# A two-layer attention, FFN, SSD and mixture-of-experts kernel on one Trainium2 core: attention in row and column tiles of TensorE, softmax sums and decay rows on ScalarE, a held expert fetch

## What is computed

```
# gate: a two-way decayed scan over the tokens of a sample (four of them: L0_cond, L0_cond2, L1_cond, L1_cond2)
decay = exp(-exp(w)) * (0.5 + 0.5 * tf)           # one number for a channel and a sample
a = a * decay + ekv_t ; b = b * decay + ek_t      # forward and backward over t
num = nf + nb - ekv + euk * vf ; den = df + db - ek + euk
out = sigmoid(r) * (num / max(den, 1e-8)) * (0.8 + 0.2 * tf)
# L0 attention: 16 heads of 16 channels, causal
att = einsum('bhtd,bhsd->bhts', q, k) / sqrt(16) + mask
z = softmax(att) @ v ;  x = x + z @ Wo.T
# L0 feed-forward: ternary weights, 8-bit activations, 256 -> 1024 -> 256
# L1 attention: an SSD (Mamba-2) block, 64 heads of 8, chunks of 32
# L1 feed-forward: 8 experts, top 2, 256 -> 704 -> 256
for e in range(8):
    h = silu(x @ w1[e].T) * (x @ w3[e].T)
    out = out + h @ w2[e].T * expert_weight
```

## Time and profile before

| | us |
|---|---|
| median of 3 runs (827.2 to 828.41) | 827.82 |
| the profiled execution | 827.53 |
| its span on the chip | 825.7 |
| start, to the first scores | about 0 to 86 |
| attention | about 86 to 304 |
| feed-forward | about 304 to 400 |
| SSD block | about 400 to 585 |
| routing and first gather | about 585 to 616 |
| experts | about 616 to 803 |
| combining and output | about 803 to 825.7 |

### The profile page before, as it was taken

One profiled execution on the slowest core, in us unless ns is written; L12 is line 12 of the kernel. 1 busy time (PEld: TensorE's weight loads), 2 busy tenths in 40 slices (PEclk: granted clock), 3 DMA queues, 4 the chain that ended last, 5 costly groups with the idle time before them and its releaser, 6 DMA issues.

```text
span 825.7 us, 13424 instructions
## 1 busy us (share of the span) xinstructions
PE 617.2 (75%) x5534; PEld 483.4 (59%) x5534; DVE 455.6 (55%) x565; ACT 329.9 (40%) x582; POOL 279.5 (34%) x150
## 2 busy tenths in 40 slices
PE   0009768986887771656799989998639999999990
PEld 0005657875786671224556456556628889898980
DVE  5995899869779729666395534443531111111113
ACT  5342234433542533767456654554312212222210
POOL 0542474564573404530001964430010212122210
PEclk9999877757879855958699999999759999999995
DMA  9200000000000000000000000000186888888814
GB/s 360 76 0 0 1 0 2 0 1 1 1 1 1 5 34 1 1 0 1 0 2 2 2 2 2 2 3 2 48 315 244 293 329 289 323 295 311 311 69 163
DMA packets 18125, 72.14 MB, mean 87 GB/s; under 512 B 4304, under 2 KB 9552, under 8 KB 14224
## 3 DMA queue, kind: packets, MB, share of 16 engines
q1 hardware_dynamic: 15856, 65.24, 21.5%
q0 software_dynamic: 2208, 6.03, 1.9%
HBM read 66.16 MB, written 5.11 MB: 86 GB/s over the span
## 4 chain that ended last, share of the span: by engine, by line
PE 56%; DVE 31%; ACT 7%; issue 3%; DMA 2%; SPq 0%; POOL 0%; DVEq 0%; POOLq 0%; ACTq 0%
PE PS L1257 46%; DVE arena L845 5%; DVE arena L846 5%; PE PS L1294 3%; DVE nmx L945 2%; PE PS L1306 1%; DVE dmat L841 1%; DVE R L863 1%; PE PS L1477 1%; DVE arena L860 1%; DVE arena L850 1%; DVE peak L1021 1%; DVE arena L1017 1%; DVE arena L1247 1%; DVE arena L859 1%
## 5 line engine op out<-in xcount | busy, mean ns | idle before, releaser
L1257 PE MATMUL PS<-arena 128*128 128x128 f32 (+5 forms) x1940 | 240.3, 293 | 35.5 <-DVE arena L934 15.1
L1257 PEld LDWEIGHTS PS<-arena 128*128 128x128 f32 (+2 forms) x1940 | 204.6, 181 | 68.4 <-issue 40.5
L549 ACT ACTIVATE arena<-PS,nmx 128x128 f32<-128x128 f32 (+1 forms) x128 | 43.4, 422 | 120.1 <-DVE nmx L945 120.1
L1234 DVE TENSOR_TENSOR R<-arena,PS 128x128 f32<-128x128 f32 x23 | 6.6, 287 | 145.4 <-ACT arena L786 145.4
L452 POOL DMA_INDIRECT ypair<-arena,oid x23 | 22.8, 990 | 146.6 <-ACT arena L792 146.6
L1257 PE MATMUL PS<-arena,R 128*128 128x256 f32 (+1 forms) x276 | 67.9, 388 | 0.6 <-ACT arena L792 0.6
L1257 PE MATMUL PS<-A,arena 128*128 128x128 f32 (+1 forms) x96 | 27.9, 446 | 38.3 <-DVE A L868 37.9
L1257 PEld LDWEIGHTS PS<-arena,R 128*128 128x128 f32 (+1 forms) x276 | 48.7, 189 | 13.3 <-issue 8.6
L1306 PE MATMUL PS<-ident,arena 128*128 128x128 f32 x192 | 34.5, 329 | 27.9 <-ACT arena L533 27.2
L426 POOL TENSOR_TENSOR arena<-arena 128x1024 f32<-128x1024 f32 x16 | 37.8, 2368 | 44.9 <-DVE arena L1089 36.9
L1294 PE MATMUL PS<-arena 128*128 128x128 f32 (+1 forms) x176 | 50.9, 417 | 0.8 <-DVE arena L887 0.8
(11 more groups left out here) (261 smaller groups left out, 1180.3 us busy)
## 6 DMA issues: line engine op xcount, KB each, us to landing
arena<-in_moe SPq DMA_DIRECT2D x23, 1408.0 KB, 6.6
arena<-in_moe SPq DMA_DIRECT2D x23, 768.0 KB, 8.2
arena<-ypair SPq DMA_DIRECT2D x4, 512.0 KB, 5.4
inproj<-in_inproj SPq DMA_DIRECT2D x1, 1344.0 KB, 11.3
arena<-in_fT SPq DMA_DIRECT2D x1, 1024.0 KB, 5.3
...
R<-in_w2T SPq DMA_DIRECT2D x1, 1024.0 KB, 10.3
```

The lines of the kernel that those rows point to most:

```text
L549: sc.activation(pr[u % 2][:, j, 0:n], PS[:, 2 * (u % 2) + j // 2, (j % 2) * 256:(j % 2) * 256 + n], ACT.Exp, bias=nmx[:, u % 2, j:j + 1]). ...
L1257: last = mm(dst, l, r, start=(n == 0), stop=(n == len(pairs) - 1))
```

## The change

Six things:
- **Scores.** GpSimd's masked copies go. ScalarE writes q twice, once with the even heads kept and once with the odd (`qT[0]`, `qT[1]`, eight copies for four). A head's scores are then a matmul over the 32 partitions that hold it and its neighbour (rows 0, 32, 64 or 96), in the order 0, 2, 1, 3, so that neighbours in the list use other rows and another bank of PSUM. The mask is two bf16 matmuls of 256 columns for four of 128.
- **Values.** v is the stationary operand, padded with zeros to 32 channels a head (GpSimd's memset), and the turned probabilities are the moving one; four heads write the four 32-partition groups of one bank. The result is z already turned: `turn_z` and `zt_copy` go. `project` has four steps of 128 padded channels for two.
- **Softmax sums.** ScalarE's exponentials write their row sums (`accum_out`). VectorE inverts them for each two units (`inverse_sums`), TensorE turns and repeats the inverses in eight column-tile matmuls, ScalarE copies them (`turned_sums`), and VectorE's `normalise`, now 16 times for 8, multiplies.
- **Decay rows.** Line 841 goes from VectorE; ScalarE writes each decay row in four instructions of 256 (`decay`), into one of two buffers.
- **Down projection.** Its last matmul has 128 rows, with zeros in the upper half.
- **Fetches.** The fetches of blocks 1 to 3 wait for the first gather to land.

```diff
@@ sync: fetches
                 if b >= RING:
                     sp.wait_ge(S["pe_y"], b - RING + 1)
+                if b == 1:
+                    sp.wait_ge(ld_xin[0], 16)
@@ gpsimd
-            masked(0)
-            masked(1)
-            for u in range(32):
-                if u + 2 < 32:
-                    masked(u + 2)
-                f, k = divmod(u, FRAME)
-                if k >= 2:
-                    gate_add(f + 2, k - 2)
-                elif k == 0 and f:
-                    gate_add(f + 1, 3)
+            pool.wait_ge(S["dve_R"], 2)
+            pool.memset(vv[:, :, :, HD:VW], 0.0).then_inc(S["pool_pad"], 1)
+            for i in range(2, 8):
+                for k in range(4):
+                    gate_add(i, k)
@@ scalar
+            def decay(i):
+                m, c = divmod(i, 2)
+                act.wait_ge(S["dve_dec"], 1)
+                if i >= 2:
+                    act.wait_ge(S["dve_scan"], 2 * (i - 1))
+                for n in range(4):
+                    ct, b = divmod(n, 2)
+                    sc.activation(dmats[i % 2][:, n * T:(n + 1) * T], notfirst[:], ACT.Copy,
+                                  scale=dec[:, m, ct, 2 * c + b:2 * c + b + 1]).then_inc(S["act_decay"], 1)
                 sc.activation(ek[:, ct, :], ek[:, ct, :], ACT.Exp).then_inc(S["act_ek"], 1)
+                decay(ct)
             bonus(0)
             bonus(1)
+            decay(2)
-                              ACT.Exp, bias=nmx[:, u % 2, j:j + 1]).then_inc(S["act_exp"], 1)
+                              ACT.Exp, bias=nmx[:, u % 2, j:j + 1],
+                              accum_out=esum[:, u // 2 % 2, 4 * (u % 2) + j:4 * (u % 2) + j + 1]).then_inc(S["act_exp"], 1)
                 if u >= 1:
                     pt_copy(u - 1)
+                if u % 2 and u >= 3:
+                    turned_sums(u // 2 - 1)
+                if k == 3 and i + 3 < 8:
+                    decay(i + 3)
@@ vector
+            def inverse_sums(p):
+                dve.wait_ge(S["act_exp"], 8 * (p + 1))
+                done(v.reciprocal(rinv[:, p % 2, :], esum[:, p % 2, :]), "dve_rinv")
+            def normalise(p):
+                dve.wait_ge(S["act_rT"], p + 1)
+                o = 256 * (p % 2)
+                done(v.tensor_tensor(zT[p // 2 % 2][:, o:o + 256], PS[:, 6 + p % 2, 0:256], rT[:, p % 2, :], ALU.mult), "dve_zn")
+                if u % 2 and u >= 3:
+                    inverse_sums(u // 2 - 1)
                 done(v.tensor_reduce(nmx[:, u % 2, :], ...), "dve_max")
+                if u % 2 == 0 and u >= 4:
+                    normalise(u // 2 - 2)
@@ tensor
+                for j in (0, 2, 1, 3):
+                    r = 32 * (2 * (g % 2) + j // 2)
+                    mm(PS[:, 2 * (u % 2) + j // 2, (j % 2) * 256:(j % 2) * 256 + n], qT[j % 2][r:r + 32, ch, ct, t:t + P],
+                       kT[r:r + 32, ct, b * T:b * T + n], start=(j % 2 == 0), stop=False)
+                for k in range(tt + 1):
+                    for j in range(4):
+                        last = mm(PS[32 * j:32 * j + 32, 6 + p % 2, o:o + P], vv[:, 2 * b + k, 4 * g + j, :],
+                                  pt[u % 2][:, (j * (tt + 1) + k) * P:(j * (tt + 1) + k + 1) * P], start=(k == 0), stop=(k == tt))
+                if u % 2:
+                    pe.wait_ge(S["dve_rinv"], p + 1)
+                    for h in range(8):
+                        j, o = h % 4, 256 + 128 * (h // 4)
+                        last = mm(PS[32 * j:32 * j + 32, 6 + p % 2, o:o + P], rinv[:, p % 2, h:h + 1].broadcast_to([P, VW]), ident[:],
+                                  start=True, stop=True)
@@ tensor: down_block
-                last = acc(bank(7, D), [(h[:, f * P:(f + 1) * P], w[:, f, :]) for f in range(5)]
-                           + [(h[0:64, 640:768], w[0:64, 5, :])])
+                last = acc(bank(7, D), [(h[:, f * P:(f + 1) * P], w[:, f, :]) for f in range(FT)])
```

174 lines of the change are left out of this document (73 added, 101 removed).

## The result

The changed kernel takes 793.2 us (median of four runs, 789.7 to 797.5) where the kernel before takes 827.5 on the same chip: a ratio of 0.959, with an interval of 0.954 to 0.965. Forecast were 805.7 us, with a range of 794 to 817: the sign was right, and the gain of 34 us is half as large again as the 22 forecast.

What follows compares the result with a forecast made beforehand. VectorE was taken to set attention's pace mostly, TensorE now and then, and TensorE alone the experts. 827.5 - 2.4 (start) - 10 (attention) - 3.2 (gather) - 6.5 (down projection) = 805.4, median 805.7 us, range 794 to 817.

Steps and rivals of the forecast that it cites:

- the attention term: Attention stage: 14 us saved on VectorE's pairs of scans and light units, 4 given back for TensorE, so -10 us.
- The 4 us given back: Attention: TensorE at half clock would still set some frames, so 4 of the 14 us saved are lost.
- the walk behind (b): Attention's light units: ScalarE's work listed between two maxima, 11.7 us, then VectorE's, putting the next maximum at 14.6 us.
- (b): Attention's three light units a frame: decay rows leave VectorE, ScalarE becomes the limit; -1.7 us a frame, -10 in all.
- Term (a): Attention's pairs of scans: without GpSimd's masked copies VectorE is delayed 0.65 us less a frame, six times: -4 us.
- the down projection: Experts: a last matmul on 128 rows instead of 64 saves 0.28 us a block, times 23: -6.5 us.
- Start: Before attention's first maximum: two early decay rows of 1.24 us leave VectorE, a second memset costs 0.1: -2.4 us.
- The frames: Attention's groups of five units: a pair with four scans takes 16 us, three light units 14 to 15 us.
- TensorE's terms (c): Attention: row-tiled scores and column-tiled values cut TensorE from about 5.5 to 3.7 us per 256-wide unit at full clock.
- First gather: Before the experts: with later weight fetches held, the gather takes 2.7 us instead of 5.95: -3.2 us.
- The slower one: Rival: TensorE stays at half clock throughout attention, 7.0 us a unit, stage 234 us for 218, total 832; chance 0.05.
- ScalarE keeps up: Rival: in attention a sum costs 0.1 us and scores are never late; attention -27, total 788; chance 0.1.

Runs made afterwards that it cites:

- copies beside: Changed kernel with GpSimd's 32 masked copies put back in their old places, written where nobody reads: 803.0 us, ratio 0.971.
- early addition: Changed kernel with VectorE's reciprocal of the sums moved behind the even unit's maximum and the addition to x ahead of its unit's maximum: 790.5 us, ratio 0.955.
- scores three times: Changed kernel with the four score matmuls of each unit run two times more into the same place: 816.5 us.
- full rows: Changed kernel with each head's scores taken over all 128 channel rows instead of its 32: 795.9 us; repeated on two later kernels: 796.2 and 781.9 us.

## Why the prediction was right in kind and short in size

**Where it failed.** The step that failed is the attention term, -10 us, where the stage gained 21.1 between the two profiles (13.9 in the loop and 7.2 behind it). Four things in it were wrong. Attention's end had no term, though the two prices of the values matmuls stood in the prediction: 7.2 us. The 4 us given back because TensorE at half clock would set some frames were not given back. And the walk behind (b) made ScalarE the limit of the light units, which taking 11.3 us from ScalarE showed it not to be. Term (a) was 4 us where the copies cost 10; this error and that of (b) cancel, since the loop gained 13.9 us for the 14 of both together. A smaller failure is the down projection, 0.28 us a block where it is 0.39.

**Start (-2.4 forecast, -4.0 measured).** The two decay rows gave their 2.5: the first gate multiplication starts at 57.61 for 60.35, of which 0.24 is an input that landed earlier. The other 1.3 lie behind it. The first eight projection matmuls took 9.3 us for 10.0, a time that varied from 8.6 to 10.2 over the profiles whatever the kernel, and the first scores 0.5 less. The projection's time is the clock's: its first records start 0.85 us apart and the later ones 0.43, and the slow ones are six in this profile of the kernel before and four in that of the changed one. By the means above the start gained 2.9. The step was right, and most of its remainder is chance between single executions.

**Attention's loop (-10 forecast, -13.9 measured).** The frames came out as drawn, pairs of 15.7 us for the 16 forecast and trios of 14.7 for 14.6, and that is luck: neither (a) nor (b) was right. Term (a) was too small: the copies' delay was read at two places of one frame and multiplied, 4 us; put back, they cost 10.0. A sum by line would have shown more of it: over the loop of the kernel before the 24 scans alone took 63.8 us, where undelayed ones of 2.29 take 55. It would have overstated it too, since the changed kernel's scans still take 59.3, beside the gates' own additions.

```profile
L845 DVE TENSOR_TENSOR_SCAN arena<-dmat,arena 128x1024 f32<-128x1024 f32 x12 | 33.0, 2750 | 0.4
L846 DVE TENSOR_TENSOR_SCAN arena<-dmat,arena 128x1024 f32<-128x1024 f32 x12 | 30.8, 2564 | 0.4
```

Term (b) had the wrong limit. The walk gave ScalarE 0.2 us for a sum; measured is 0.09 (11.3 us over 128 exponentials), the read of 0.19 lying beside the next exponential. The changed kernel's rows:

```profile
151.87 0.47 ACT L544 ACTIVATE arena<-PS,nmx 128x256 f32<-128x256 f32 x1 [3.68 <-DVE nmx L942]
152.24 0.19 ACT L544 ACTIVATION_READ_ACCUMULATOR arena<-PS,nmx 128x1 f32 x1
152.33 0.46 ACT L544 ACTIVATE arena<-PS,nmx 128x256 f32<-128x256 f32 x1
```

(152.33 - 151.87 = 0.46, where four took 1.57 before, 0.37 from one to the next.) And the time didn't move with it. Behind both stands the step of the 4 us: 14 us of gain, of which TensorE at half clock was to give 4 back. Next to nothing was given back. Over five kernels that differ in VectorE's load, the loop less VectorE's busy time stays within 2.4 us, less than the 25.2 to 29.0 over four executions of the same attention code:

| kernel | loop, us | VectorE busy | idle |
|---|---|---|---|
| before | 197.1 | 171.1 | 26.0 |
| before, decay rows on ScalarE | 187.6 | 162.5 | 25.1 |
| changed, copies beside | 193.2 | 166.5 | 26.7 |
| changed, decay rows on VectorE | 188.0 | 163.3 | 24.7 |
| changed | 183.2 | 156.1 | 27.1 |

So the right sum was VectorE's own: decay rows -9.7 (six of 1.62), less delay of the other instructions -9.6 (scans -4.5, step 5 -3.1, step 4 -2.0), the new reciprocals and multiplications +4.1 (the prediction had them at under 4, inside its bounds and not in its sum), together -15. That TensorE's 30 us less brought nothing is read from these idle times; no run takes the masked copies out of the kernel before and leaves its TensorE work. Nor does the rule go further than these five: with the early addition the idle time fell to 23.4 us, and with the scores three times it rose to 47.0.

**Attention's end (no term, -7.2 measured).** The prediction priced the values matmuls at 1.86 and 3.44 us and never carried them to the one place where nothing hides them. It is the largest omission. How much of the end is the clock's own can be read from the other kernels: built on the changed one, it is 11.0 to 11.4 us at a clock of 1.00 and 13.8 to 14.5 at 0.78 to 0.80, with nearly the same instructions; built on the kernel before, 17.0 to 18.6 at 0.62 to 0.68.

**TensorE's terms (c).** Row tiles were taken at 0.9 us for four heads and measured 1.07; values at 0.46 measured 0.46 to 0.64. The Trainium skill (TensorEngine Tiling, Array Packing; section Key Properties) says that a change of tiling mode drains TensorE, and was set against this part of the change. The down projection's blocks agree: 0.39 us for two changes, more than the 0.28 taken. What the changes cost in attention is not shown: full rows take those of the row tiles away and leave the loop as long, but at another clock.

**First gather (-3.2 forecast, -3.0 measured).** 2.92 us for 5.95. In the five profiles with the fetches of the kernel before it took 5.95 to 7.1, in the fourteen with held ones 2.8 to 2.9. Block 1 didn't wait for its weights: with the 128-row matmul in both, the blocks come at the same distances with and without the hold.

**Down projection (-6.5 forecast, -9.0 measured).** The term was mis-sized. 0.28 a block was an estimate from the switch into the smaller array, doubled and then shaded down; it is 0.39, 23 times.

**Rivals.** The slower one, TensorE at half clock throughout, didn't happen, though its mechanism has a grain of truth: the clock did fall, from 0.77 to 0.72, and not by the lower load alone, as full rows bring it to 0.85. "ScalarE keeps up" was the nearest in size (788), and right about ScalarE.

**Left open.** The feed-forward and SSD stages took 305.6 to 307.3 us in the five profiles built on the kernel before and 306.8 to 311.9 in the fourteen built on the changed one, in code that is the same; the means are 306.4 and 309.8. So some 3 us of the gain are given back there, more than the 0.9 of the table. About 2 of them lie in the SSD block, whose instructions are the same in both. There TensorE stands still at places where the profile shows nothing that it waits for: four times, 4.6 to 5.0 us together, in the five kernels, and six or seven times at other places, 4.9 to 6.9 us, in the fourteen. Why is not known, nor how much of those 2 us it is. Why row tiles come with a lower clock is open as well, and so is how attention's end would go with the old values at full clock; the split of its 5.6 us above is an estimate.
